# Streaming the window-attention layers: one continuous slot pipeline, with each feed-forward step right behind the query-key projection

## What is computed

```python
x = x + 0.5 * window_stack(layernorm(x))
x = x + latent_attention(layernorm(x))
x = x + 0.5 * window_stack(layernorm(x))     # same weights

def window_stack(x):
    for i in range(6):
        x = attn_layer(shift_tokens(x), Wqkv[i], q_scale[i], k_scale[i], Wo[i]) + x
        x = ffn_layer(shift_tokens(x), ln_g[i], ln_b[i], W1[i], b1[i], W2[i], b2[i]) + x
    return x
```

## Time and profile before

| | us |
|---|---|
| median of 3 runs | 6235.63 |
| lowest, highest | 6224.58, 6290.46 |
| the profiled execution | 6207.84 |
| its span, first to last instruction | 6205.9 |
| TensorE busy in the span | 5338.6 (86%) |
| VectorE busy | 4233.8 (68%) |
| ScalarE busy | 3441.8 (55%) |
| GpSimd busy | 3247.6 (52%) |
| mean granted TensorE clock | 0.92 of 2.4 GHz |

### The profile page before, as it was taken

The page is one execution under the profiler, slowest core; times in us unless marked ns, Lnnn a source line. Parts: engine busy times, 40 slices in busy tenths (PEclk is TensorE's granted clock), DMA queues, the critical chain, the costliest instruction groups (busy, mean ns, idle before and its releaser), DMA issues. The chain is left out here.

```text
span 6205.9 us, 145869 instructions
## 1 busy us (share of the span) xinstructions
PE 5338.6 (86%) x46548; PEld 3093.3 (50%) x46548; DVE 4233.8 (68%) x8735; ACT 3441.8 (55%) x10596; POOL 3247.6 (52%) x3718
## 2 busy tenths in 40 slices
PE   6978889889898896699999997988979889798898
PEld 4645546456465563243433343655646546455464
DVE  6858868588586883244444445867858778587685
ACT  4747747577475772022222233766747657477574
POOL 5848748478484782100000003856838658487483
PEclk8999999999899997589888897999989999999999
DMA  2111111111111111000000001111111111111110
GB/s 64 40 38 41 39 40 40 39 40 41 38 40 39 41 40 25 0 1 1 1 1 1 1 1 45 41 43 36 40 37 41 47 31 41 37 42 40 37 40 26
DMA packets 246571, 197.52 MB, mean 32 GB/s; under 512 B 73980, under 2 KB 242456, under 8 KB 243992
## 3 DMA queue, kind: packets, MB, share of 16 engines
q1 hardware_dynamic: 246296, 193.82, 12.1%
HBM read 41.61 MB, written 1.05 MB: 7 GB/s over the span
## 5 line engine op out<-in xcount | busy, mean ns | idle before, releaser
L507 POOL TENSOR_TENSOR rot<-t 128x512 f32<-128x512 f32 x768 | 972.7, 1266 | 799.0 <-DVE t L774 788.8
L685 ACT ACTIVATE prob<-ps,nmx,inv 128x96 f32<-128x96 f32 x3072 | 1281.1, 427 | 22.6 <-DVE nmx L769 14.0
L511 POOL TENSOR_TENSOR inv<-ssm,neg_half 128x8 f32<-128x8 f32 x768 | 1269.5, 1653 | 0.0
L537 PE MATMUL ps<-w_qkv,xs 128*128 128x512 f32 x1536 | 888.6, 663 | 110.7 <-DVE xs L790 53.8
L678 ACT COPY pt<-ps 96x512 f32<-96x512 f32 x768 | 447.2, 582 | 789.5 <-PE ps L573 789.5
L1274 ACT ACTIVATE ptl<-ps_l 128x1024 f32<-128x1024 f32 (+1 forms) x288 | 281.4, 977 | 903.7 <-PE ps_l L1149 672.1
L580 PE MATMUL ps<-ident,rot 128*128 128x128 f32 x3072 | 499.6, 286 | 306.4 <-POOL rot L515 304.7
L758 DVE TENSOR_REDUCE mx<-ps 128x4 f32<-128x384 f32 x768 | 427.7, 557 | 341.2 <-PE ps L564 337.0
L783 DVE TENSOR_SCALAR ssm<-ss 128x8 f32<-128x8 f32 x768 | 630.2, 821 | 26.3
L685 ACT ACTIVATION_READ_ACCUMULATOR prob<-ps,nmx,inv 128x1 f32 x3072 | 609.8, 199 | 0.0
L774 DVE TENSOR_TENSOR t<-ps,tab_s 128x256 f32<-128x256 f32 x1536 | 571.3, 411 | 0.2
(11 more groups left out here) (203 smaller groups left out, 8431.4 us busy)
## 6 DMA issues: line engine op xcount, KB each, us to landing
vs<-vt SPq DMA_DIRECT2D x768, 96.0 KB, 2.2
vs<-vt SPq DMA_DIRECT2D x768, 64.0 KB, 2.0
vs<-vt SPq DMA_DIRECT2D x768, 32.0 KB, 1.8
w_qkv<-in_L_ffn_Wqkv SPq DMA_DIRECT2D x12, 1536.0 KB, 6.5
w_o<-in_L_ffn_Wo SPq DMA_DIRECT2D x12, 512.0 KB, 7.2
w<-in_L_ffn_W SPq DMA_DIRECT2D x12, 341.0 KB
wcos<-const_wc SPq DMA_DIRECT2D x2, 1024.0 KB, 4.9
wsin<-const_ws SPq DMA_DIRECT2D x2, 1024.0 KB, 7.3
```

The lines of the kernel that those rows point to most:

```text
L507: nc.gpsimd.tensor_tensor(rot[:, n % 4], t1[:, n % 2], t2[:, n % 2], ALU.add).then_inc(z["rotated"], 1)
L511: nc.gpsimd.tensor_tensor(inv[:, n % 4], ssm[:, n % 2], neg_half[:, 0:2 * HU], ALU.pow).then_inc(z["inv_ready"], 1)
L537: pe.matmul(ps[:, s % 2, :], xs[:, s // UT, :], w_qkv[:, 0:2, u * 256:(u + 1) * 256], start=True, stop=True).then_inc(z["qk_ready"], 1)
L685: e = nc.scalar.activation(prob[:, n % 2, h, :], scores[:, h % 2, h // 2, :], ACT.Exp, scale=inv[:, n % 4, h:h + 1], bias=nmx[:, n % 2, h: ...
```

## The change

The six layers of a stack become one stream of 384 slots. Unit j = 0 of the next layer follows unit 63 directly: `walk` unrolls the 64 slots of a layer, once for the first, once in a loop over the other five, and ends with 20 slots of draining. The table of positions loses its 17th tile.

The feed-forward stage is cut into 13 steps, p = 0 to 12, one a slot; `feed` gives the step and the group. A group starts when its four tiles have passed the output projection, and 3 of 16 slots have no step. On TensorE the step stands directly behind the query-key projection of the slot and ahead of the output projection, mask and scores. All steps use one PSUM bank (`ff`, bank 7); for that, attention outputs move to the second half of bank 6 behind the values. The gate chunks are projected first and copied out with their bias (steps 5 to 8), one gelu over 128x1536 follows, and then come the other chunks, each multiplied at once (9 to 11), and the down-projections (12).

Within a slot, TensorE projects the values ahead of turning `prob` and `rot`; GpSimd does the power ahead of the addition; ScalarE copies `ots` first and `vt` in the same slot as the projection. The projection weights are loaded in four parts behind the last four units of a layer; output weights, scales and feed-forward weights have a semaphore and a slot of their own.

```diff
+        f_gate = sb("f_gate", [P, len(CH), GT])
+        hm = sb("hm", [P, len(CH), GT])
+        ff = ps[:, 7, :]
+        HV = slice(256, 512)
...
+        def feed(j, part):
+            g, p = divmod(j - LAG_Y, 16)
+            return (p, g - 1) if p <= 12 and not (part == "first" and g < 1) else (None, None)
...
+        def walk(eng, slot):
+            for j in range(UNITS):
+                slot(0, j, "first")
+            with eng.Fori(1, DEPTH) as L:
+                for j in range(UNITS):
+                    slot(L, j, "steady")
+            for j in range(UNITS, UNITS + LAG_Y + 13):
+                slot(DEPTH - 1, j, "last")
...
+            def layer(L, part):
+                for j in range(UNITS):
+                    if part != "first":
+                        if j == LAG_Y:
+                            sp.wait_ge(z["y_ready"], (L + L0) * TILES)
+                            output_weights(L)
+                        if j == LAG_Y + 16:
+                            sp.wait_ge(z["x_a_ready"], (L + L0) * G + 1)
+                            feed_forward_weights(L)
+                    if j == UNITS - 6:
+                        sp.wait_ge(z["tab_ready"], 2 * tile_no(L, TILES - 1))
+                        attention_scales(L if part == "last" else L + 1)
...
+                    if j >= UNITS - UT and part != "last":
+                        projection_weights(L + 1, j % UT)
...
+            def feed_forward(L, p, g):
+                if p == 1:
...
+                    pe.matmul(ff, mean_w[:, :], f_src[:, :], start=True, stop=True).then_inc(z["mean_ready"], 1)
+                if p == 2:
+                    pe.wait_ge(z["ln_squared"], qn + 1)
...
+                if 5 <= p <= 7:
...
+                    if m == 0:
+                        pe.wait_ge(z["ln_ready"], gn + 1)
...
+                    else:
+                        pe.wait_ge(z["gate_read"], gn * 3 + m)
+                    pe.matmul(ff[0:w], w_1[:, INNER + lo:INNER + lo + w], f_xn[:, :], start=True, stop=True).then_inc(z["gate_up"], 1)
...
+                if 9 <= p <= 11:
...
+                        pe.wait_ge(z["prod_ready"], gn * 3 + m)
+                    pe.matmul(ff[0:w], w_1[:, lo:lo + w], f_xn[:, :], start=True, stop=True).then_inc(z["up_ready"], 1)
+                if p == 12:
+                    pe.wait_ge(z["prod_ready"], gn * 3 + 3)
...
+                if live(LAG_V):
...
+                    if had(LAG_O, 1):
+                        pe.wait_ge(z["ot_read"], done(LAG_O, 1))
+                    pe.matmul(ps[:, 6, 0:256], xs[:, n // UT, :], w_qkv[:, 2, (n % UT) * 256:(n % UT + 1) * 256],
+                              start=True, stop=True).then_inc(z["v_ready"], 1)
...
+                if p is not None and 6 <= p <= 8:
+                    act.wait_ge(z["gate_up"], group_no(L, g) * 3 + m + 1)
+                    nc.scalar.activation(f_gate[0:w, m, :], ff[0:w], ACT.Identity, bias=vec[0:w, 6 + m:7 + m]).then_inc(z["gate_read"], 1)
...
+                if p == 8:
+                    act.wait_ge(z["gate_read"], group_no(L, g) * 3 + 3)
+                    nc.scalar.activation(f_gate[:, :, :], f_gate[:, :, :], ACT.Gelu).then_inc(z["gelu_ready"], 1)
```

More of the change, by code:

```diff
@@ L138, in macaron_kernel @@
         x_res = sb("x_res", [P, T])
-        x_a = sb("x_a", [P, 1 + T + P])
+        x_a = sb("x_a", [P, 1 + T])
         x_b = sb("x_b", [P, 1 + T])
@@ L361, in window_stack @@
         ots = sb("ots", [P, 8, 2, P])
[L362 to L366, removed]
+        f_src, f_xc, f_sq, f_xn, f_sc = (sb("f_" + n, [P, GT]) for n in ("src", "xc", "sq", "xn", "sc"))
+        f_gate = sb("f_gate", [P, len(CH), GT])
+        f_var = sb("f_var", [P, GT // P])
+        f_rstd = sb("f_rstd", [P, GT // P])
@@ L392, in live, with clock @@
+        def clock(L, j, part):
             def live(lag):
-                return {"first": s >= lag, "steady": True, "last": s < lag}[part]
+                return {"first": j >= lag, "steady": True, "last": j - lag < UNITS}[part]
             def had(lag, back):
-                return part != "first" or s - lag - back >= 0
+                return part != "first" or j - lag - back >= 0
             def done(lag, back=0):
-                return (L + L0) * UNITS + pair * 8 + (s - lag - back + 1)
+                return (L + L0) * UNITS + (j - lag - back + 1)
@@ L457, in _ @@
+            for u in range(UT):
+                projection_weights(0, u)
             attention_scales(0)
+            output_weights(0)
             feed_forward_weights(0)
-            sp.wait_ge(z["consts_ready"], 8 + 4 * (k + 1))
-            with sp.Fori(1, DEPTH) as L:
-                layer_values(L - 1)
-                sp.wait_ge(z["y_ready"], (L + L0) * TILES)
-                attention_weights(L)
-                sp.wait_ge(z["tab_ready"], (L + L0) * (2 * TILES + 2))
-                attention_scales(L)
-                sp.wait_ge(z["x_a_ready"], (L + L0) * G + 1)
-                feed_forward_weights(L)
@@ L468, in _ @@
-            layer_values(DEPTH - 1)
+            sp.wait_ge(z["consts_ready"], 8 + 2 * (k + 1))
+            layer(0, "first")
+            with sp.Fori(1, DEPTH - 1) as L:
+                layer(L, "steady")
+            layer(DEPTH - 1, "last")
         @block.gpsimd
@@ L474, in _ @@
             nc.gpsimd.memset(vt[:, :, :, :], 0.0).then_inc(z["consts_ready"], 1)
[L475 to L477 removed]
+            nc.gpsimd.memset(f_gate[:, :, :], 0.0).then_inc(z["gate_clear"], 1)
+            pool.wait_ge(z["consts_ready"], 8 + 2 * (k + 1))
             pool.wait_ge(z["const_in"], 64 + 32 * (k + 1))
[L479 to L519 removed]
@@ L522, in _ @@
+            pool.wait_ge(z["sc_in"], (L0 + k + 1) * SC)
+            scaled_tables(0, 0)
+            walk(pool, slot)
         @block.tensor
         def _(pe):
[L524 to L650 removed]
@@ L653, in _ @@
+            walk(pe, slot)
         @block.scalar
         def _(act):
[L655 to L726 removed]
@@ L850, in copy_on_pool @@
+            dve.wait_ge(z["ln_scaled"], q0)
+            shifted(0, 0)
+            walk(dve, slot)
 def copy_on_pool(nc, dst, src, zeros):
```

681 lines of the change are left out of this document (313 added, 368 removed).

## The result

The changed kernel takes 6390.33 us in the median of 4 runs (6379.24 to 6437.38); the kernel before took 6256.42 us in 4 runs on the same chip (6224.58 to 6290.46). The ratio is 1.0228, with a 95% interval of 1.0145 to 1.031: the change makes the kernel slower. The profiled execution took 6379.24 us, the one of before 6207.84: 171 us more. The medians lie 134 us apart; the profiled execution of before was faster than any of those four.

The account below looks back on a forecast made before the run. GpSimd's chain was taken to bound the slots, with 82.4 us a layer of feed-forward and filling to win. Per stack 1928 + 23 x 16.4 + 50 + 15 + 20 = 2390 us against 2364.5, giving 6273 us; range 6095 to 6430.

Parts of the forecast that it names:

- The third rival: An activation behind a table load waits as long again as the load's 1.28 us: 118 us more, 6391 us; chance 0.08.
- The slot without feed-forward work: Attention slots carrying no step: 4.68 us plain, 6.05 with output projection, four in 20.1; a stack pays 1928 us instead of 1870.
- The rival that it costs nothing: Value projection ahead of the turning falls in TensorE's idle time; plain slots stay under 4.45 us, total 6106 us; chance 0.27.
- The slots with feed-forward work: Slot lengths where TensorE's step stands before the scores and its waits delay them: 4.7 to 8.35 us, 16.4 us a group.
- step 3: Slot with nothing of the feed-forward work on TensorE, but with the output projection: 6.05 us.
- step 2: Variance on TensorE, waiting for the square after ScalarE's small copy: 4.80 + 0.63 + 0.9 = 6.3 us.
- step 11: Slot with a TensorE product after VectorE is through its slot, plus the output projection: 3.79 + 0.75 + 0.9 + 1.78 = 7.2 us.
- The gelu: One ScalarE instruction of 1.4 us with two table loads of 1.28 us a group; its slot takes 8.35 us.
- The turn of the loop: Engines may stop as the layer loop goes back: 3 us for each of five turns, 15 us a stack.
- the fourth rival: Next layer's weights or bias vectors land late, so feed-forward steps don't overlap: up to 110 us over 6273; chance 0.06.
- The tail: End of a stack: 15.7 us of draining and one feed-forward group alone, taken as 34: 50 us.
- The clock as a rival: Gaps at the gelu drop TensorE to 1.2 GHz for about two slots: 4 us a group, total 6417 us; chance 0.14.

## Why the prediction was right or wrong

The forecast of 6273 us was 117 us too low, and the time lies in the range, on the slower side. The way was right and the size was not: 0.6% slower was forecast, 2.3% was measured. The loop, the waits and the gelu that it named are what the runs show; the clock's place and one path were wrong. About 20 of the 117 us aren't the change's: the median of the kernel before was 6236 in the three runs that the forecast started from, and 6256 in the four that it is compared with. The third rival's 6391 us is the measured time almost to the microsecond, by accident: the runs refute its mechanism. The sizes, in the order of the prediction's steps:

- *The slot without feed-forward work*: right. 4.68 us were forecast and measured, 6.05 and 6.17 with the output projection; four slots take 20.2 us where 20.1 were forecast. The value projection alone, in the kernel before, reproduces slot and wait. The rival that it costs nothing, given 0.27, was wrong by its own test: plain slots did not stay under 4.45 us. The power's move was priced at 0.21 us a slot by itself; the run on it gave about 0.2 us a slot and 2.1%. That agreement holds for the average alone: plain slots gained 0.1 us, slots with an output projection 0.5. The prediction read one plain slot, of 4.39 us; six of them in a row take 4.19 to 4.75 us, 4.38 on average, so that the one it read happened to be typical.
- *The slots with feed-forward work*: ten of the twelve lengths within 0.13 us. (The terms of step 1 add up to 6.0, not to the 6.1 that it gives; 6.18 was measured.) The step that failed first is step 3, "nothing on TensorE, output projection, 6.05": it measured 7.21, 7.39 on average, because in the slot behind the wait of 1.49 us at step 2 the clock is at 1.2 GHz. The prediction had looked for the clock's loss at the gelu, priced apart, and not behind a wait that it had itself worked out. The second is step 11, "3.79 + 0.75 + 0.9 + 1.78": VectorE is not through its slot at 3.79 but has two copies to make first, 0.86 us in this trace. The prediction doesn't name them; they stand on the path in one slot of a group. Of the 0.86 us, 0.37 come of the power's move on GpSimd.
- *The group*: 96.7 forecast, 99.1 typical, 99.8 on average without turns of the loop. That is 3.1 us more, over 23 groups 71 us a stack; 20 us had been set aside for the clock, and the other 51 are about the whole of the 47 us by which a stack was longer than the 2390 forecast.
- *The gelu*: right where the clock holds. 1.4 us against 1.48, a slot of 8.35 against 8.48. The third rival, an activation that waits behind a load, is out; the rows are shown below.
- *The turn of the loop*: 3 us for each of five turns a stack were forecast. Only four cost anything, those inside the loop; from the first layer, which stands before the loop, into it, and from the loop into the last slots the slots keep their length to within 0.2 us. A group with one of the four takes 103.0 us on average, 3.2 more than the others, which makes 13 us a stack against 15. Late weights, the fourth rival, did not come: no load stands before a wait of the steady stretch.
- *The tail*: 50 us forecast. From the last S of the 384 slots to the last x_a it takes 63 and 64 us; about 8 of them are the last steps of the group before, which makes 56.
- *The clock as a rival*: the mechanism was right, place and price wrong. It costs about 1.7 us a group where 4 were priced: 1.2 at step 3, where it was not looked for, 0.3 on average at step 10, where it was, and 0.2 at steps 2, 6 and 7, where it falls in single groups.
- *Outside the sum*: the latent attention, 32 us longer at 0.79 instead of 0.81 of the clock. The prediction took unchanged code for unchanged time. Why its clock was lower isn't shown by any run here; as the other runs have 0.76 to 0.80, the kernel before with one edit among them, it was chance that the trace of before had 0.81.

The whole balance of the two stacks in the profiled execution, in us: no stage and no filling, 12 x 82.4 = 989 saved. Paid: 46 groups whose 12 steps lengthen the slots by 18.1 (99.1 less four times 20.24), 834, and which are 0.7 longer than the typical one on average, 34; 48 groups whose own slots take 81.0 instead of 77.9, 146; two tails, 112; eight turns, 26. The first four slots of each stack are short, 14 us instead of 20, which gives back 12. That makes 151 where 144 were measured.

Where did the expected gain go, then? Into TensorE's place for the step. Steps of the feed-forward network wait for ScalarE and VectorE of the slot before, which finish them last; placed ahead of the scores, every such wait is a wait of S, and S is on the loop that sets every slot. 18.1 us a group fell by 11 when only this place was changed, and the kernel became 6.6% faster than the one before. So streaming was right, and its order gave the whole gain back.

## What to carry to other kernels

In a software pipeline whose slot is closed by a loop over several engines, added work belongs where the engine has slack behind the loop's last product, and where its inputs have had time to come; here the kernel with the same instructions ahead of the loop's first product took 9.5% more time (by the two ratios, 1.0228 and 0.9342). Move one instruction and write the loop down again on paper: half a microsecond in front of the turning cost 2.5%, though TensorE was 86% busy and had no more to do. And where two edits come together, time each: one of these was worth 2.1%, and the other hid it.

## What was unexpected of the hardware

A table load cost its 1.28 us and hardly more. ScalarE at the gelu, and then the first instructions behind a turn of the layer loop on TensorE and VectorE:

```profile
825.04 0.58 ACT L719 COPY qkt<-ps 128x512 f32<-128x512 f32 x1
825.63 1.28 ACT L725 ACT_TABLE_LOAD   x1
826.93 1.48 ACT L725 ACTIVATE f_gate<-f_gate 128x1536 f32<-128x1536 f32 x1
...
828.43 1.97 PE L593 MATMUL ps<-w_qkv,xs 128*128 128x512 f32 x2 [4.51 <-issue]
828.67 0.18 DVE L782 RECIPROCAL rec<-sums 128x4 f32<-128x4 f32 x1 [4.00 <-issue]
```

The load begins 0.01 us after the end of the copy and the gelu 0.02 us after the end of the load. The Trainium skill (ScalarE: Activation LUTs, What ACT_TABLE_LOAD costs) adds a drain of some 1.38 us to each load. Neither these rows nor the 2.84 us for two switches leave room for it here.

At the eight turns of the layer loop TensorE issues nothing for 3.5 to 5.0 us, though the profile shows nothing that it waits for. By the lengths of groups with and without a turn it costs 3.2 us net; what the time goes into wasn't tried.

The wait of 1.49 us at step 2 took the granted clock of the next 3.5 us to 0.65. A wait of 1.55 us in the slot of step 7 did not: around and behind it, from 1113 to 1120 us, the clock is 1.00. It is no rule for the group either: the clock fell behind step 2 in 45 of 46 groups, in the slot of step 7 in 4 of 46, and behind the 2.32 us at the gelu in 15 of 36. With the first wait filled by five products the clock stayed at 1.00. What tells these waits apart is left open; no run tried it.

A copy of 64x128 on VectorE (L736) takes 0.59 us beside GpSimd's scaling of 128x256 elements, in 190 copies, and 0.22 us beside GpSimd's power of 128x8, in 192.
